# Graph network on one Trainium2 core: the repeated search of a diffusion repair under a flag of each tile

## The reference

```python
def _top_p_attention(X, W1, W2, W3):
    q = X @ W1.T @ W2.T
    k = X @ W3.T
    logits = q @ k.T / TAU
    probs = jax.nn.softmax(logits, axis=-1)
    idx = jnp.argsort(-probs, axis=-1)
    sp = jnp.take_along_axis(probs, idx, axis=-1)
    cs = jnp.cumsum(sp, axis=-1)
    keep_sorted = cs - sp < TOP_P
    ...
    A = probs * mask
    return A / jnp.maximum(A.sum(-1, keepdims=True), 1e-12)

for n in range(STEPS):                      # STEPS = 2
    A = _top_p_attention(Xa, W1, W2, W3)
    Xf = R @ Xf
    Xa = A @ Xa
    Z = Z + Xf @ U1[n].T + Xa @ U2[n].T
```

## Time and profile before

| | |
|---|---|
| median of 3 runs | 2990.27 us (2988.0 to 2992.92) |
| profiled execution | 2988.41 us |
| its span | 2986.7 us |
| mean granted TensorE clock | 0.895 of full speed |
| TensorE busy | 2314.8 us (78%) |
| VectorE busy | 1941.0 us (65%) |
| ScalarE busy | 1224.8 us (41%) |
| GpSimd busy | 662.2 us (22%) |

### The profile page before, as it was taken

The page is one execution under the profiler, slowest core; times in us unless marked ns, Lnnn a source line. Parts: engine busy times, 40 slices in busy tenths (PEclk is TensorE's granted clock), DMA queues, the critical chain, the costliest instruction groups (busy, mean ns, idle before and its releaser), DMA issues. The chain is left out here.

```text
span 2986.7 us, 44231 instructions
## 1 busy us (share of the span) xinstructions
PE 2314.8 (78%) x14310; PEld 1703.0 (57%) x14310; DVE 1941.0 (65%) x4668; ACT 1224.8 (41%) x1981; POOL 662.2 (22%) x1649
## 2 busy tenths in 40 slices
PE   3499999589536999996844974877563599999999
PEld 2377777377315787775523763766462244444468
DVE  5567777523337877777238888888965577777741
ACT  3455566211346666661256863766422100000000
POOL 2000000200224444340025643555402200000000
PEclk9699999899768999998966987989787799999999
DMA  1322221054100000000100000000004000000013
GB/s 46 119 98 97 97 81 68 5 191 145 42 17 13 19 23 19 22 27 14 48 17 6 16 11 11 16 11 16 11 11 155 2 1 0 0 0 0 0 50 96
DMA packets 49299, 120.85 MB, mean 40 GB/s; under 512 B 5952, under 2 KB 24672, under 8 KB 45792
## 3 DMA queue, kind: packets, MB, share of 16 engines
q1 hardware_dynamic: 49120, 118.83, 11.8%
HBM read 93.85 MB, written 24.97 MB: 40 GB/s over the span
## 5 line engine op out<-in xcount | busy, mean ns | idle before, releaser
L1923 DVE SCALAR_TENSOR_TENSOR fil_acc<-bank,fil_node,fil_acc 128x256 f32<-128x256 f32 x682 | 330.0, 484 | 110.4 <-PE bank L1991 97.8
L1346 PE MATMUL bank<-idf,X 128*128 128x128 f32 x968 | 136.2, 302 | 202.9 <-DVE step_recips L1841 202.9
L1436 ACT ACTIVATE step_PT<-bank 128x512 f32<-128x512 f32 (+1 forms) x264 | 127.5, 577 | 357.4 <-PE bank L1346 357.4
L1989 PE MATMUL bank<-parts_in,fil_xTh 128*128 128x512 f16 x704 | 268.5, 381 | 0.0
L1991 PE MATMUL bank<-parts_in,fil_xTl 128*128 128x512 f16 x704 | 268.3, 381 | 0.0
L1990 PE MATMUL bank<-parts_in,fil_xTh 128*128 128x512 f16 x704 | 268.2, 381 | 0.0
L1346 PEld LDWEIGHTS bank<-idf,X 128*128 128x128 f32 x968 | 119.4, 154 | 215.4 <-DVE step_recips L1841 206.2
L722 PE MATMUL bank<-V,HL 128*128 128x256 f32 x968 | 236.4, 386 | 0.2
L1356 PE MATMUL bank<-kH,qHL 128*128 128x512 f16 (+1 forms) x264 | 105.9, 401 | 151.9 <-ACT step_E L1445 117.7
L1378 PE MATMUL bank<-A,step_PT 128*128 128x256 f32 x968 | 216.1, 379 | 0.0
L1378 PE MATMUL bank<-H,step_PT 128*128 128x256 f32 x968 | 216.0, 379 | 0.0
(11 more groups left out here) (382 smaller groups left out, 5044.4 us busy)
## 6 DMA issues: line engine op xcount, KB each, us to landing
gat_A<-in_adj SPq DMA_DIRECT2D x22, 1408.0 KB, 5.9
step_a<-adjT SPq DMA_DIRECT2D x44, 352.0 KB, 3.0
gcn_raw<-in_L_W SPq DMA_DIRECT2D x16, 512.0 KB, 4.7
split<-gcn_halves SPq DMA_DIRECT2D x16, 512.0 KB, 3.4
parts_in<-split SPq DMA_DIRECT2D x4, 2048.0 KB, 19.2
adjT<-gat_a SPq DMA_DIRECT2D x22, 352.0 KB, 2.3
gcn_a<-adjT SPq DMA_DIRECT2D x22, 352.0 KB, 3.9
out_a<-adjT SPq DMA_DIRECT2D x22, 352.0 KB, 2.9
```

The source lines that it names most:

```text
L1346: last = pe.transpose(p_bank[n % nb][:, i * 128:i * 128 + 128], M[j][:, (b + i) * 128:(b + i) * 128 + 128], core.idf[:])
L1436: act.activation(PT[:, b * 128:(b + m) * 128], p_bank[n % len(p_bank)][:, 0:m * 128], ACT.Copy).then_inc(pT_done, 1)
L1923: c(dve.scalar_tensor_tensor(out=acc[k][:], in0=ps, scalar=node[k][:, n:n + 1], in1=acc[k][:], op0=ALU.mult, op1=ALU.add))
L1989: pe.matmul(w_bank[n % 4][:], xTh[k][:, x], wh[:, blk], start=c == 0, stop=False)
```

## The change

`fresh`, which says for each row of each tile whether the answer is missing, is copied to columns 6 and 7 of the flags, so that `flag_any` has an element for each tile. `flat` and `flag_any` grow from 6 to 8 rows. In `again` the search, the sort, the replacing of answers and the forming of `M` stand inside a branch on the tile's own flag. The secant step before it is still done for both tiles, and the second `verify` too.

```diff
-        flags, flagsT, flat = sb("flags", [128, 32]), sb("flagsT", [128, 32]), sb("flat", [6, 128])
-        flag_any = sb("flag_any", [6, 1], I32)
+        flags, flagsT, flat = sb("flags", [128, 32]), sb("flagsT", [128, 32]), sb("flat", [8, 128])
+        flag_any = sb("flag_any", [8, 1], I32)
...
                 s(dve.tensor_tensor(flags[:, 1:2], fresh[:, 0:1], fresh[:, 1:2], ALU.max))
+                s(dve.tensor_copy(flags[:, 6:8], fresh[:]))
                 s.after()
...
-                    s(dve.tensor_copy(flat[:, 32 * g:32 * g + 32], flagsT[32 * g:32 * g + 6, :]))
+                    s(dve.tensor_copy(flat[:, 32 * g:32 * g + 32], flagsT[32 * g:32 * g + 8, :]))
...
                 for j in range(2):
-                    candidates(p, q, j)
-                threshold(q, fresh, (0, 1))
-                s = steps(extra)
-                s(dve.copy_predicated(answer[q][:], wrong[:], fresh[:]))
-                s.after()
-                for j in range(2):
-                    at_or_above(s, p, q, j, column(answer[q], j), kept)
-                s.after()
+                    with dve.If(raised(6 + j) > 0):
+                        candidates(p, q, j)
+                        threshold(q, fresh, (j,))
+                        s = steps(extra)
+                        s(dve.copy_predicated(column(answer[q], j), wrong[:, j:j + 1], column(fresh, j)))
+                        s.after()
+                        at_or_above(s, p, q, j, column(answer[q], j), kept)
+                        s.after()
                 verify(q, valid)
```

## The result

The changed kernel takes 2984.91 us (median of 15 runs, 2981.69 to 2988.14), beside 2991.43 us for the kernel before in the same comparison: ratio 0.9972, 95% interval 0.9965 to 0.9979. That is 6.5 us less by the two medians and 8.4 us by the ratio, which is the measure used from here on. The forecast was 2963 and a range of 2956 to 2976. The sign is right, and the size is a quarter to a third of the 27 us foretold. The profiled execution has a span of 2983.2 us, 3.5 under that of before.

A forecast was written before the change was run, and what follows sets the result against it. Neither engine bounds the repairs; TensorE waits for VectorE's `settle`. Savings of 8.7 us in step 0 and 19.8 in step 1, less 1.1 for copies, give 27.4: 2961.0 profiled, 2962.9 median, range 2956 to 2976.

The forecast's parts named there:

- The path: In `again`, TensorE and ScalarE stand waiting for VectorE, so each microsecond removed there comes off the program.
- The price of a single tile's repair: Search, closing pass and sort of one tile spared in `again`: 8.7 us saved in step 0, 9.9 per step 1 repair.
- The two tests: Flag tests added inside `again`, one true (0.7 us) and one false (1.3): 2.0 us a repair, bounds 1.6 and 4.0.
- The assumption that in each pair one tile alone was raised: In all three pairs running `again`, only one tile has its flag; chance 0.79, total saving 27.4 us.
- double pair: Rival: both tiles raised in one repaired pair; 6.2 us more in step 1 instead of 9.9 less, total 2979; chance 0.10.
- the far jumps: Rival: tests in ordinary pairs jump over longer `again` code and wait for fetches; 16 us of gain lost, 2979; chance 0.06.
- Step 0's gaps, taken as hidden: Step 0's checks outside the repaired pair are off the path, since TensorE does not wait for VectorE's reciprocals there.
- The check: One copy of 128x2 into the flags in every `verify`: 0.07 us each, 15 on the path, 1.1 us.
- eight rows: Four copies into `flat` and the reduction read 8 rows instead of 6, at no cost.
- the masked row: Rival: a row formerly mended by its partner's repeat goes to `general`, adding about 140 us, 3103; chance 0.03.
- The clock: TensorE's clock: shorter idle before step 0's transposes gives back some tenths of a microsecond at most; nothing in step 1.
- such mixtures: Double pair and far jumps occurring together, which could end within the 6 us indistinguishable from no difference.

The follow-up runs named there:

- code of the old length: Changed kernel with the 11 tie instructions per tile removed from the end of never-executed `general`: 2975.26 us, ratio 0.9941 to the kernel before.
- 11 dead copies: Kernel before plus 11 never-executed small copies per tile at the end of `general`, 22 per pair: 2995.22 us, ratio 1.0009.
- 40 dead copies: Kernel before plus 40 never-executed small copies per tile at the end of `general`: 3007.99 us, ratio 1.0047.

## Why the prediction was wrong, point by point

**The path.** Right for the three repairs: the stretches' changes reached the program's time (10.0 and 9.4 us of the 10.1 and 9.8 in step 1, 5.8 of 5.7 in step 0).

**The price of a single tile's repair.** Right: 9.9 us saved was foretold for step 1, 10.1 and 9.8 measured. The two tests cost 2.1 us in each repair, where 2.0 was foretold: in front of the mask and of the second check 0.24 and 0.23 us became 0.95 and 1.64 in the first repair of step 1, whose first tile is the raised one, and 2.15 and 0.44 in the last, whose second tile is:

```profile
1837.31 3.04 DVE L1584 SCALAR_TENSOR_TENSOR step_low<-step_E,step_final 128x2709 f32<-128x2709 f32 x1 [0.95 <-DVE step_final L1774]
...
2143.00 3.04 DVE L1584 SCALAR_TENSOR_TENSOR step_low<-step_E,step_final 128x2709 f32<-128x2709 f32 x1 [2.15 <-issue]
...
2159.72 0.16 DVE L1665 TENSOR_TENSOR step_need<-step_kept,step_answer 128x2 f32<-128x2 f32 x1 [0.44 <-DVE X L1648]
```

**The assumption that in each pair one tile alone was raised.** This step failed, in step 0. Instead of 8.7 us saved the stretch grew by 5.7. The sum was mis-sized by 14.4 us here. The price of a double pair was right (6.2 foretold for step 1; 5.7 in step 0, 6.5 and 6.9 when it was forced in step 1); its chance was drawn from rarity, as if the tiles of a pair were independent, and nothing in the trace bore on it.

**The code's length.** The second failed step. I gave the far jumps a chance of 0.06 and a size of 16 us as an alternative to the double pair, where they are a term of every version of the sum. With the double pair put right the sum is 13.0 us saved (27.4 less 14.4), and 6.5 to 8.4 were measured, so some 5 to 6 us are left for this term, which the sum put at nothing. The same executed work in code of the old length ran 0.0031 faster, 9 us, and saved 18 in all. So the term has either sign, and a size of some 5 us for changes of this length. The Trainium skill (Runtime: NRT & Kernel Launch, "Instruction fetch mechanics") says that a taken jump to a target outside the held pages waits for a fetch. I argued from its page size that twenty instructions move few targets. The runs don't bear that argument out: 22 unexecuted instructions a pair moved the gaps from 61.9 to 70.3 us, and more or less of such code changed the packets of instructions from 112 to 125 and 99. On the wait itself the trace agrees with the page: each of the 165 dear gaps has a packet of q14 that starts inside it, and the short gaps of the same tests mostly have none.

**Step 0's gaps, taken as hidden.** Only partly. TensorE doesn't wait for the reciprocals there, but ScalarE waits for VectorE, and TensorE waits for ScalarE. ScalarE's waits in step 0: for the reciprocals, before it writes the next exponentials, in the changed kernel; and for the largest entries (`step_top`), which VectorE takes behind `settle`, in the kernel before and in the one without `general`:

```profile
ACT step_E L1445 <- DVE step_recips L1842: 3.0, 2, 2.8
...
ACT step_nm L1452 <- DVE step_top L1580: 24.3, 11, 6.8
...
ACT step_nm L1452 <- DVE step_top L1580: 13.4, 6, 3.2
```

The second wait is the larger one and shrinks by 10.9 us, and without `general` the kernel before was 9.2 us ahead by the ninth pair of step 0. I had followed TensorE's wait for VectorE and not ScalarE's.

**The rest.** The check grew by 0.09 us (0.07 foretold), and eight rows cost as much as six. `general` never ran, and 48 closing passes exclude the masked row. The clock gave nothing back; at the end of step 1 it took some: the restart of TensorE's transposes behind 3.41 us of idle time lasts 3.96 us, where it was 2.82 behind 2.94. From 2223 to 2227 us the mean granted clock is 0.65 of full speed, between its two levels (1.2 and 2.4 GHz), where it was 1.00 at this place before (2229 to 2232), and the products behind (L1378) start 1.5 us later for it. The double pair alone, at 2977 to 2979, lay just outside the range; both rivals together gave 2985. I had named such mixtures, but drawn the range as if they couldn't happen.

**What stays open.** The sum of the gaps in front of `settle`'s last step doesn't move in step with the time (70.3 us with 11 dead copies, which lost 2.7 us; 69.7 in the changed kernel), because other gaps move the other way, as at L1557. All of VectorE's idle time from 860 to 2262 us that no other engine ends (in front of instructions marked issue or remote, or behind the reduction of the flags), without the repaired stretches, does better. Together with the stretches it comes within 2.6 us of the time of all eleven experiments and of the changed kernel; differences from the kernel before, us:

| kernel | idle time | with the stretches | by the ratio |
|---|---|---|---|
| changed | +3.9 | -10.3 | -8.4 |
| 11 dead copies | +3.2 | +3.4 | +2.7 |
| 40 dead copies | +16.7 | +16.3 | +14 |
| before, without `general` | -19.7 | -20.1 | -19 |
| changed, without `general` | -15.2 | -30.1 | -29 |
| changed, old length | -0.5 | -15.1 | -18 |

Why that holds although some of step 0's idle time is hidden is not shown. Which jump finds its target at hand was not worked out from the addresses of the code, and padding to move a target was not tried.

## What to carry to other kernels

A branch that spares work in a rare case is paid for in every case that jumps over it: count the instructions that are jumped over, not only those that run, and take the reserve code out or make it short first. Before splitting a joint repair by a flag of its parts, count how often the parts are raised together, by a counter in the kernel or from the data; rarity is no evidence of independence. When an unrolled program changes length, expect shifts of some microseconds of either sign beside the effect, and hold the length fixed in one control. Look for packets of the instruction queue inside an idle time that no engine ends.

## What the runs showed of the hardware

A test of a flag in memory by VectorE, from the reduction that makes it to the next instruction, takes 0.94 us where the branch isn't jumped and 1.3 us where it is. Two false tests take 2.1 us, mostly 3.7 where VectorE waits for a fetch of instructions, and 6.1 where it waits for two: one such wait is about 1.6 us or a little more. Eighty never executed instructions for each pair cost 14 us over 22 pairs, about 0.6 us a pair, and removing a never executed repair with its test (64 instructions a pair) gained 19. The Trainium skill's figure for a compare and branch (Advanced Engine Details and Errata, "Control Flow Timing", about 108 ns) covers the smallest part of that.
